# A graph kernel on Trainium2: GpSimd zeroes a small tile ahead of each gather of edge rows, and waits for it

## The reference

```python
# layer 0, graph part
agg_h = jax.ops.segment_sum(feat_n[src], dst, num_segments=N)
agg_e = jax.ops.segment_sum(edge_feat, dst, num_segments=N)
rst = jnp.concatenate([agg_h, agg_e], axis=1) @ weight
...
# layer 1, graph part
messages = edge_val[:, None] * embeddings[edge_src]
neighbor_emb = jax.ops.segment_sum(messages, edge_dst, num_segments=embeddings.shape[0])
...
# both layers
xn = _layernorm(x, axis=-1)
x = x + graph(xn, src, dst, ...) + mix(xn[None], ...)[0]
x = x + experts(_layernorm(x, axis=-1)[None], ...)[0]
```

## Time and profile before

| | |
|---|---|
| time of three runs, median (lowest to highest) | 2390.33 us (2377.59 to 2392.18) |
| profiled execution: span from first to last instruction | 2408.5 us |
| PE, PEld busy | 77%, 60% |
| DVE, ACT, POOL busy | 52%, 29%, 38% |
| gathers of L650, first and last start | 67.6 and 1889.3 us |

### The profile page before, as it was taken

One profiled execution on the slowest core, in us unless ns is written; L12 is line 12 of the kernel. 1 busy time (PEld: TensorE's weight loads), 2 busy tenths in 40 slices (PEclk: granted clock), 3 DMA queues, 4 the chain that ended last, 5 costly groups with the idle time before them and its releaser, 6 DMA issues. The chain is left out here.

```text
span 2408.5 us, 34947 instructions
## 1 busy us (share of the span) xinstructions
PE 1864.4 (77%) x10583; PEld 1445.5 (60%) x10584; DVE 1245.5 (52%) x3264; ACT 705.9 (29%) x1624; POOL 908.1 (38%) x933
## 2 busy tenths in 40 slices
PE   6598568667385999999936876558889884699975
PEld 4365346445263999999923454335566572588875
DVE  6553676667474444444474644542344376433345
ACT  5122333333431111111156710111222132133324
POOL 0555464656120222222203245446566200245442
PEclk9999688889696999999977988768899997699997
DMA  7454443444353111101143133223333226312124
GB/s 231 133 136 127 116 118 98 125 119 123 124 218 116 33 32 33 32 32 33 30 134 102 37 105 90 71 84 98 97 115 112 63 75 255 142 61 64 63 57 146
DMA packets 171237, 239.46 MB, mean 99 GB/s; under 512 B 74146, under 2 KB 139262, under 8 KB 168693
## 3 DMA queue, kind: packets, MB, share of 16 engines
q0 software_dynamic: 42336, 112.74, 16.7%
q1 hardware_dynamic: 116884, 113.45, 14.4%
q10 hardware_dynamic: 11904, 11.96, 1.6%
HBM read 184.86 MB, written 56.12 MB: 100 GB/s over the span
## 5 line engine op out<-in xcount | busy, mean ns | idle before, releaser
L650 POOL DMA_INDIRECT agg_message<-table,edges_src x638 | 623.8, 978 | 641.6 <-PE agg_partial L713 205.4
L2817 PEld LDWEIGHTS ex_p_h<-ex_xT,ex_own_up 128*128 128x128 f32 (+1 forms) x2464 | 281.4, 192 | 2.7 <-issue 1.3
L2817 PE MATMUL ex_p_h<-ex_xT,ex_own_up 128*128 128x128 f32 (+1 forms) x2464 | 282.1, 276 | 1.0 <-DVE ex_xT L2868 1.0
L2872 DVE COPY ex_own_up<-moe_up 128x1280 f32 x114 | 100.5, 882 | 168.8 <-PE ex_p_h L2817 168.0
L2776 POOL DMA_INDIRECT ex_x<-moe_in,route_token_at x58 | 57.3, 988 | 312.1 <-PE ex_p_x L2807 242.3
L709 PE MATMUL agg_partial<-agg_message,moe_up 128*64 128x321 f32 x638 | 115.0, 487 | 47.9 <-issue 14.1
L2860 ACT ACTIVATE ex_gate_h<-ex_p_h 128x640 f32<-128x640 f32 x56 | 39.5, 705 | 315.3 <-PE ex_p_h L2817 315.3
L3013 ACT COPY ex_own_up<-moe_up 128x1024 f32 x66 | 67.5, 1044 | 215.4 <-PE ex_p_h L2986 169.8
L2942 POOL DMA_INDIRECT ex_x<-moe_in,route_token_at x66 | 64.4, 975 | 169.7 <-PE ex_p_x L2973 87.3
L2986 PEld LDWEIGHTS ex_p_h<-ex_xT,ex_own_up 128*128 128x128 f32 x1024 | 118.8, 195 | 12.4 <-issue 10.6
L2986 PE MATMUL ex_p_h<-ex_xT,ex_own_up 128*128 128x128 f32 x1024 | 123.4, 280 | 3.4 <-issue 1.2
(11 more groups left out here) (665 smaller groups left out, 3701.0 us busy)
## 6 DMA issues: line engine op xcount, KB each, us to landing
moe_up<-in_f_w SPq DMA_DIRECT2D x8, 1386.0 KB
agg_message<-in_edge_rows SPq DMA_DIRECT2D x54, 192.0 KB
agg_message<-table,edges_src POOLq DMA_INDIRECT x638
sums<-agg_span SPq DMA_DIRECT2D x107, 80.2 KB
moe_up<-in_f_w SPq DMA_DIRECT2D x4, 2048.0 KB, 14.6
moe_down<-in_f_w SPq DMA_DIRECT2D x4, 2048.0 KB
sums<-agg_span SPq DMA_DIRECT2D x107, 64.0 KB
moe0b_down<-in_f_w SPq DMA_DIRECT2D x8, 768.0 KB
```

What stands on the lines that cost most here:

```text
L650: pool.indirect_dma_start(out=to[:, k * w:k * w + D], out_offset=None, in_=self.table, in_offset=bass.IndirectOffsetOnAxis(ap=self.edges.s ...
L2817: return pe.matmul(to, own_up[:, o:o + n], xT[:, k * D + c * P:k * D + (c + 1) * P], start=(c == 0), stop=(c == 1))
L2872: dve.tensor_copy(own_up[:, a:b], at(up, e * U0 + a, b - a)).then_inc(up_copied, 1)
```

## The change

A tile `rest` of 128x128 f32 (64 KiB of SBUF over all partitions) and a semaphore `paused` are added to `EdgeSums`. Before each gather POOL writes zeros to `rest`, and the gather waits until that is done. Nothing reads `rest`. The wait's value is the number of tiles gathered so far in this layer, and one.

```diff
--- before.py
+++ after.py
@@ -615,7 +615,9 @@
         self.onehot = m.sb("onehot", [P, self.ring * GE * W]) if onehot is None else onehot
         self.shift = m.sb("shift", [P, self.ring * P])
         self.span = m.sb("span", [P, 2 * width])
+        self.rest = m.sb("rest", [P, P])
         self.partial = m.ps("partial", [P, 512])
+        self.paused = m.sem("paused")
         self.gathered, self.featured = ([m.sem(f"{n}{k}") for k in range(ring)] for n in ("gathered", "featured"))
         self.counting, self.marked, self.shifted, self.used, self.moved, self.stored = (
             m.sem(n) for n in ("counting", "marked", "shifted", "used", "moved", "stored"))
@@ -645,8 +647,10 @@
         if g >= self.ring:
             pool.wait_ge(self.used, g - self.ring + 1)
         to, w = self.slot(self.message, g, self.width), self.width
-        for k in self.tiles(g):
+        for n, k in enumerate(self.tiles(g)):
             t = self.place(g) + k
+            pool.memset(self.rest[:, :], 0.0).then_inc(self.paused, 1)
+            pool.wait_ge(self.paused, self.place(g) - HEAD + n + 1)
             pool.indirect_dma_start(out=to[:, k * w:k * w + D], out_offset=None, in_=self.table,
                                     in_offset=bass.IndirectOffsetOnAxis(ap=self.edges.src[:, t:t + 1], axis=0))\
                 .then_inc(self.gathered[g % self.ring], 16)
```

## The result

The changed kernel takes **2278.16 us** (median of four runs, 2264.00 to 2284.89) against 2384.43 us of the kernel before on the same chip: a ratio of 0.9545, 95% interval 0.9501 to 0.9589. It is 4.5% faster, some 106 us, where 7 us slower was forecast. The profiled execution spans 2282.8 us, 125.7 us less than the one before.

A forecast was written before the change was run, and what follows sets the result against it. PE was taken to set the pace, POOL having 0.33 and 0.36 us spare per gather; 0.37 us added would cost 5.8 us in layer 0 and 1.6 in layer 1, +7.4 on 2390.33: 2397.7 us, range 2376 to 2470.

The forecast's parts named there:

- fifth rival: Gather stages: spread gathers leave room in DMA queues, PE's and ACT's small waits shrink, kernel gets faster; chance 0.05.
- The room: Time per gather before PE waits: 1.60 us in layer 0, 1.66 in layer 1, leaving 0.33 and 0.36 us to add.
- price per further 0.1 us: Cost over both layers once the addition per gather exceeds the spare time: 14.4 + 16.2 = 31 us.
- The sum of the cycle: POOL's added time per gather, two gaps and memset less today's 0.30 us, plus 0.03 for DVE: 0.37 us.
- gap A: POOL, from end of a gather to start of the memset: taken as 0.16 us, between 0 and 0.30.
- gap B: POOL, from end of the memset to start of the gather waiting for it: taken as 0.28 us, between 0.16 and 0.40.
- The 0.03 us for memsets that meet DVE: Added per gather for memsets locked out of the shared SBUF port by two-port DVE operations, about 16% of layer 1's time.
- third rival: Layer 0's mixer: DVE reciprocals of 3353 ns hold the memset back, addition 0.72 us, time 2448 us; chance 0.06.
- The slow restart: Any waiting gather restarts 0.89 us late, as a scatter does: addition 0.95 us, about 2575 us; chance 0.06.
- The cover: Claimed gone: addition 0.45 us or over, PE waits for gathers late in both stages, 2437 to 2468 us; chance 0.28.
- Rival four: The memset fits into the 0.30 us between gathers or adds under 0.33 us: next to no effect, 2390 us; chance 0.28.

The follow-up runs named there:

- e10_slot224: Changed kernel with one awaited memset of 224 columns, in the buffer the gather then fills, in place of 128: 2283.61 us, ratio 0.9523 to the kernel before.
- e9_mixed64: Changed kernel with two memsets, of 1 and 64 columns, each waited for, ahead of every gather: 2298.61 us, ratio 0.9591 to the kernel before.

## Why the prediction was wrong

**The reading of the bound failed.** The prediction stated that only later gathers stand behind POOL's wait and only PE waits for them. Its fifth rival, the faster one, spoke of spread gathers that ease DMA queues, and was put at 0.05 because "nothing shows PE waiting for a gather in these stages; 1% would be 24 us of waits that I do not see". PE did stand idle, 143 us in layer 1's stage alone (24 with plain DMAs), not for gathers but for ACT and DVE, which in turn stood with PE's results done and unannounced. The late signals are a term that the sum put at nothing; they measure 523 us of late release, and taking half of them away was worth 106 us. The fifth rival had the direction and the shrinking waits of PE right, but its reason, room in the DMA queues, is the one that the quarter of the bytes refuted. The rows were there: the earlier trace rows has a gather held for 3.13 us by "remote", and the earlier trace rows 14.7 us of it. The earlier trace rows was also misread. Of POOL's 641.6 idle us before gathers PE's products ended 205.4, a third and not "most"; 169.9 us are the 0.30 us between gathers. I read a releaser that isn't named as noise.

**The room was measured against a PE that the gathers slowed.** The 1.60 and 1.66 us per gather came from stretches in which PE was held up itself. In the changed kernel PE is faster and POOL runs without slack for long pieces of layer 1, such as these 27 gathers, 1.449 us apart (timeline of POOL):

```profile
1559.79 0.95 POOL L654 DMA_INDIRECT agg_message<-table,edges_src  x1 [0.27 <-POOL agg_rest L652]
...
1597.47 1.63 POOL L654 DMA_INDIRECT agg_message<-table,edges_src  x1 [0.27 <-issue]
```

PE loses little by it there; over the whole run its waits that end with a gather's landing are few (total, times, longest):

```profile
PE agg_partial L713 <- DMA agg_message<-table,edges_src: 14.4, 6, 4.0
```

But a price per further 0.1 us of 31 us was too low; between 1.522 and 1.597 us it is 56 us, as if some 560 of the 638 gathers counted instead of 306.

**The sum of the cycle.** Forecast 0.16 + 0.20 + 0.28 - 0.30 + 0.03 = 0.37 us. Measured: gap A 0.00 to 0.01 (304.11 to 304.12), memset 0.22, gap B 0.27, so 0.49 - 0.30 = 0.19 us. The memset starts right behind a gather, the low end of its range; that term was over by 0.16 us. Gap B was right, from ACT and POOL waiting for one product. The 0.03 us for memsets that meet DVE were too much, but the effect exists: 39 of the 638 memsets took over 0.23 us and up to 0.54, each of them beside a TENSOR_SCALAR of DVE, in all 4.2 us or 0.007 us per gather. Beside the reciprocals none was held, which is against the third rival; two took 0.22 us beside one that runs from 310.46 to 313.81. The Trainium skill, page "SBUF — State Buffer", section "SBUF: two separate sides", has GpSimd and a two-port DVE operation lock each other out; the trace agrees with that if these TENSOR_SCALARs are such operations and the reciprocal is not, and no row tells an operation's mode.

```profile
253.65 1.66 DVE L1137 TENSOR_SCALAR moe_up<-moe_up,mix_bn_scale,mix_bn_shift 128x640 f32<-128x640 f32 x3 [0.15 <-issue]
253.85 0.54 POOL L652 MEMSET agg_rest<- 128x128 f32 x1
```
```profile
310.46 3.35 DVE L1170 RECIPROCAL mix_den<-mix_den 128x512 f32<-128x512 f32 x1
```
```profile
311.35 0.22 POOL L652 MEMSET agg_rest<- 128x128 f32 x1
...
312.79 0.22 POOL L652 MEMSET agg_rest<- 128x128 f32 x1
```

**The rivals.** The slow restart of 0.89 us (second) did not come. The cover (first) holds for the change's 0.19 us. It is used up at about 1.52 us: from 1.522 to 1.544 us the time already rises by 15 us (e10_slot224, e9_mixed64). Rival four was right that 0.19 us fit into the room, but it put the time at 2390 us. The page "Perfetto Trace Analysis" of the Trainium skill, section "GPSIMD Engine Instruction", wants spacing in place of spans, by which the prediction would have taken 0.14 us for the memset. Here the spans held: from 1 to 128 to 224 columns the memset's median goes from 0.11 to 0.22 to 0.30 us, and the spacing from 1.333 to 1.445 to 1.522 us, the same steps.

## What to carry to other kernels

When engines wait while nothing named is late, put the end of the producer beside the start of the consumer and ask which engine is busy whenever the two lie microseconds apart; "remote", "issue" and a DMA that the line doesn't read are such places. Room measured on a schedule is valid only as long as what slows the schedule stays. Where POOL issues indirect gathers back to back beside matmuls, try a short instruction between them that the gather waits for directly, in two or three lengths: here 0.08 us more from gather to gather brought 1.3%, 0.19 to 0.27 us 4.5 to 4.8%, and 0.46 us only 0.7%; 0.19 us without the direct wait brought 2.8%.

## What the runs showed of the hardware

- Signals of PE reached ACT, DVE and POOL up to 11 us behind PE's modelled end while POOL issued indirect gathers 1.25 us apart, and the semaphore's increment itself is on record late; ACT's signals to DVE and DVE's to ACT in the same stages passed within 0.14 us. It falls as the indirect DMAs move apart (523 us of late release at 1.25, 244 at 1.445, none from 1.6 us on), not with fewer bytes or rows, and plain DMAs on the same queue do not cause it (none at 0.54 us, none at 1.21). At 1.443 us without a direct wait it is 375 us. What in the indirect form does it was not found.
- PE was held inside groups of matmuls that wait for nothing, 19 times over 0.5 us at 1.25 us from gather to gather and once at 1.445.
- A memset of POOL (0.22 us) took up to 0.54 us beside TENSOR_SCALARs of DVE and kept its 0.22 us beside a reciprocal of 3.35 us.
- An indirect gather costs POOL 0.98 us for 128 rows and 0.94 us for 64; a plain DMA of 128 rows 0.55 us.
- A gather waiting for a memset starts 0.27 us behind its end, one behind an unawaited memset 0.16 us, and a memset starts as soon as a gather ends.
- A semaphore increment and a wait for it ahead of each gather made the kernel 1.0% slower with the spacing unchanged. Why is open.
